# Adding the expert rows by accumulating gathers instead of a gather and an addition on VectorE

## The reference, cut to what matters

```python
x = x + gat_with_relations(layernorm(x), src, dst, edge_type)     # L0 gnn
x = x + ffn0(layernorm(x))     # the argmax expert of 32: relu(relu(x W1 + b1) W2 + b2)
x = x + gnn1(layernorm(x))
x = x + ffn1(layernorm(x))     # the top 2 of 8 experts

def gnn1(x, edge_index):       # only the first n edges count, one per node
    xt = (x @ weight).reshape(n, 4, 64)
    row, col = edge_index
    alpha = softmax(leaky_relu(alpha_l(xt[row]) + alpha_r(xt[col])), axis=1)
    tmp = einsum('nh,nhd->nd', alpha[:n], xt[col[:n]])
    return broadcast(tmp over the 4 heads)
```

## Time and profile before

| | us |
|---|---|
| median of 3 runs | 3166.9 (3164.47 to 3168.32) |
| the profiled execution | 3159.72 |
| its span | 3158.1 |
| VectorE busy | 1782.5 (56%) |
| Pool busy | 1590.8 (50%) |
| TensorE busy | 2201.9 (70%) |
| ScalarE busy | 1326.0 (42%) |

### The profile page before, as it was taken

How to read it: one execution, slowest core, us unless ns; L and a number is a source line. 1 busy time by engine, 2 the same in 40 slices (tenths; PEclk the granted TensorE clock), 3 DMA queues, 4 the chain that set the end, 5 groups by cost and what they waited for, 6 DMA issues and landing times. The chain is left out here.

```text
span 3158.1 us, 49641 instructions
## 1 busy us (share of the span) xinstructions
PE 2201.9 (70%) x13093; PEld 1863.9 (59%) x13094; DVE 1782.5 (56%) x4090; ACT 1326.0 (42%) x2973; POOL 1590.8 (50%) x1585
## 2 busy tenths in 40 slices
PE   7999966777777777777628069620700099999998
PEld 6888855565666555565517057410700088888887
DVE  2411026777777777776585524656753456556564
ACT  3444445555655555565402025310211444444443
POOL 0047337777777777777450443657047033333433
PEclk8999977888888888887765569765555599999999
DMA  6456466777765555555724135632212622222331
GB/s 187 152 194 232 186 220 200 210 211 205 213 178 144 145 145 143 143 145 131 73 83 119 53 118 176 144 66 51 83 61 101 235 42 47 49 47 45 48 50 24
DMA packets 213447, 402.41 MB, mean 127 GB/s; under 512 B 46139, under 2 KB 141096, under 8 KB 206639
## 3 DMA queue, kind: packets, MB, share of 16 engines
q0 software_dynamic: 84864, 206.63, 27.9%
q1 hardware_dynamic: 127278, 193.40, 18.8%
q10 hardware_dynamic: 1168, 0.79, 0.1%
HBM read 247.26 MB, written 155.68 MB: 128 GB/s over the span
## 5 line engine op out<-in xcount | busy, mean ns | idle before, releaser
L788 POOL DMA_INDIRECT sum_ring<-h_tab,gnn_edge_row x880 | 840.3, 955 | 267.9 <-issue 260.6
L1049 PE MATMUL sum_bank<-sum_ring,sum_one_hot 128*128 128x264 f32 x1760 | 580.7, 494 | 208.8 <-issue 191.7
L1049 PEld LDWEIGHTS sum_bank<-sum_ring,sum_one_hot 128*128 128x128 f32 x1760 | 418.1, 247 | 327.1 <-issue 222.5
L1875 POOL DMA_INDIRECT out_dram<-moe_y,moe_to_node x112 | 186.6, 1666 | 383.1 <-ACT moe_y L1901 352.1
L699 PE MATMUL rows_bank<-rows_w_rows,rows_xnT 128*128 128x264 f32 x1568 | 363.0, 391 | 6.8 <-ACT rows_h_rows L495 6.7
L699 PEld LDWEIGHTS rows_bank<-rows_w_rows,rows_xnT 128*128 128x128 f32 x1568 | 298.1, 193 | 56.7 <-ACT rows_h_rows L495 7.6
L838 ACT ACTIVATE sum_distance_by_lane<-all_iota,gnn_minus_local 128x128 bf16<-128x128 f32 x880 | 267.4, 386 | 0.1
L904 DVE TENSOR_TENSOR sum_ring<-sum_ring,sum_bank 128x1024 f32<-128x1024 f32 x220 | 265.7, 1209 | 0.4 <-ACT sum_ring L852 0.4
L1038 PEld LDWEIGHTS sum_bank<-gnn_dst_half,sum_one_hot_T 128*128 128x128 f32 x1760 | 229.9, 208 | 42.8 <-issue 39.3
L1038 PE MATMUL sum_bank<-gnn_dst_half,sum_one_hot_T 128*128 x1760 | 235.0, 292 | 27.1 <-ACT sum_one_hot_T L831 14.4
L2033 PE MATMUL moe_bank<-moe_w_low,moe_hidden_high 128*128 x896 | 244.4, 273 | 0.0
(11 more groups left out here) (408 smaller groups left out, 4164.2 us busy)
## 6 DMA issues: line engine op xcount, KB each, us to landing
h_tab<-rows_h_rows SPq DMA_DIRECT2D x49, 1056.0 KB, 3.9
sum_local_rows<-local_tab SPq DMA_DIRECT2D x110, 256.0 KB, 3.8
sorted<-sum_blank_row SPq DMA_DIRECT2D x49, 387.0 KB
moe_stage<-in_L_ffn_W_dram SPq DMA_DIRECT2D x16, 1024.0 KB
moe_tile<-sorted POOLq DMA_DIRECT2D x58, 258.0 KB, 4.2
sum_ring<-h_tab,gnn_edge_row POOLq DMA_INDIRECT x880, 3.8
sorted<-sum_zero SPq DMA_DIRECT2D x49, 256.0 KB
mask_tab<-rows_masks POOLq DMA_DIRECT2D x7, 1560.0 KB, 7.2
```

The lines of the kernel that those rows point to most:

```text
L788: nc.gpsimd.indirect_dma_start(ring[:, t % (RING * ST), :], None, k.h_tab, bass.IndirectOffsetOnAxis(k.edge_row[:, t:t + 1], 0)).then_inc( ...
L1049: last = nc.tensor.matmul(sum_b[j][:, 0:W0], hot[:, m % 2, t, :], ring[:, m % RING * ST + t, :], start=(u == 0), stop=(u == G - 1))
L1875: nc.gpsimd.indirect_dma_start(a["out"], bass.IndirectOffsetOnAxis(to_node[:, n % 2, h:h + 1], 0), y[:, n % 2, h, :], None, bounds_check=N ...
```

## The change

The buffer `y`, the semaphore `node_ok` and VectorE's `add` are gone. The gather writes to `k.x` itself, with `compute_op=ALU.add`, and is held back by the statistics of the tile eight before it. The statistics wait for the gather's semaphore.

```diff
-        y = s.sb("expert_rows", [P, SLOTS, D])
...
             for t in range(NT):
                 m = P if t < NT - 1 else TAIL
                 if t >= SLOTS:
-                    pool.wait_ge(node_ok, t - SLOTS + 1)
-                nc.gpsimd.indirect_dma_start(y[0:m, t % SLOTS, :], None, k.ys0, bass.IndirectOffsetOnAxis(k.rows0[0:m, t:t + 1], 0)).then_inc(brought[t % SLOTS], 16)
+                    pool.wait_ge(stat_ok, t - SLOTS + 1)
+                nc.gpsimd.indirect_dma_start(k.x[0:m, t, :], None, k.ys0, bass.IndirectOffsetOnAxis(k.rows0[0:m, t:t + 1], 0),
+                                             compute_op=ALU.add).then_inc(brought[t % SLOTS], 16)
...
-            def add(t):
+            def stats(t):
                 v.wait_ge(brought[t % SLOTS], 16 * (t // SLOTS + 1))
-                m = P if t < NT - 1 else TAIL
-                nc.vector.tensor_tensor(k.x[0:m, t, :], k.x[0:m, t, :], y[0:m, t % SLOTS, :], ALU.add).then_inc(node_ok, 1)
-
-            def stats(t):
-                v.wait_ge(node_ok, t + 1)
                 nc.vector.bn_stats(k.stats[:, t, :], k.x[:, t, :]).then_inc(stat_ok, 1)
...
-            add(0)
-            for t in range(1, CH):
-                add(t)
-                stats(t - 1)
-            stats(CH - 1)
+            for t in range(CH):
+                stats(t)
             variance(0)
...
-                if more:
-                    add(t1)
-                    add(t1 + 1)
                 scales(c)
                 for j in range(CH):
                     normalise(t0 + j)
                     if more:
-                        if j + 2 < CH:
-                            add(t1 + j + 2)
                         stats(t1 + j)
```

More of the change, by code:

```diff
@@ L1478, in attend1 @@
         brought = [s.sem(f"expert_rows_gathered{u}") for u in range(SLOTS)]
-        node_ok, stat_ok, var_ok, sd_ok, dve = (s.sem(n) for n in ("x_summed", "stats_ready", "var_ready", "sd_ready", "dve"))
+        stat_ok, var_ok, sd_ok, dve = (s.sem(n) for n in ("stats_ready", "var_ready", "sd_ready", "dve"))
         xn_ok, t_ps, t_ok, xt_ps = (s.sem(n) for n in ("xn_ready", "xnT_in_psum", "xnT_ready", "products_in_psum"))
```

## The result

The changed kernel takes 3178.59 us in the median of 9 runs (3172.0 to 3190.59), the kernel before 3166.9 in the median of 9 (3152.49 to 3168.32). The ratio is 1.0048, 95% interval 1.0034 to 1.0062: slower by 11 to 20 us. Predicted was 3177.5, +10.6, range 3162 to 3188. The profiled executions span 3158.1 and 3176.4 us. I write H for the time from Pool's first expert gather to its first gather of the second half: 101.2 us before (1979.09 to 2080.32), 118.9 after. That is 17.6 of the 18.3 us between the two spans. H is read from one profiled execution of each kernel; two such readings of the changed kernel, on two chips, are 118.9 and 117.9 (experiment 9), so a difference of about 1 us in H means little.

What follows compares the result with a forecast made beforehand. Pool's gather issue was to bound the stage at 1.905 us per gather; gather 48's issue, landing and 2.0 us to the root put the last root +10.6 later. Added to the 3166.9 median: 3177.5 us, range 3162 to 3188.

Steps and rivals of the forecast that it cites:

- Pool's price: In the first half of `attend1`, Pool's issue of an adding gather takes 1.605 us, against 0.95 for a plain one.
- Pool sets the pace: From chunk 2 on the gathers, 1.905 us each on Pool, set the pace and everything else follows.
- The wait for the root: VectorE's waits for ScalarE's square root, six times and 8.4 us together before, would be gone.
- VectorE's additions bring nothing: Removing 49 additions, 20.6 us of VectorE, takes 2.5 us off the path at today's pace; the gain shows nowhere.
- The landing of the last gather: Gather 48, issued at 2070.5, lands 4.2 us later at 2074.7.
- From the last root to the end: From the last chunk's square root to the end of the half, 14.25 us, nothing changes.
- the dip: Longer TensorE idling between chunks can leave it at 1.2 GHz; price 1.7 us, inside Pool's slack except in the last chunk.
- The sum: Last square root of the half at 2076.7 against 2066.07: +10.6 us, median 3177.5; chance 0.52.
- my own range: Main forecast with 1.55 to 1.67 us on Pool and a landing of 3.7 to 5.5: +7 to +15.
- 1: Pool's issue stays near plain price, 0.95 to 1.25 us, and DMA keeps up: -2.5 us, 3164.4; chance 0.26.
- rival 2: Issue cheap, but DMA engines have twice the work per row, 1.84 us per tile: +7.5, 3174.4; chance 0.10.
- 3: DMA engines pay as for the adding scatter plus contention, 2.23 us per tile: +26, 3193; chance 0.12.

Runs made afterwards that it cites:

- experiment 9: Changed kernel unedited, on a chip where the kernel before takes 3567 us: median 3579.7 against 3567.4, ratio 1.0008, H 117.9.
- experiment 7: Kernel before with a bounds check on its plain expert gathers, on a slower chip: H 116.1, no ratio given.
- experiment 4: Kernel before with gathers adding into its zeroed ring, VectorE's additions kept: ratio 1.0066, H 120.3.
- experiment 2: Changed kernel with gathers that overwrite the node rows instead of adding: ratio 0.9995, H 97.0.
- experiment 1: Changed kernel with the last tile's 106 rows gathered in two parts of 96 and 10: ratio 1.0050, H 114.1.
- 3: Changed kernel with gathers not adding and a Pool memset of 480 columns before each: ratio 1.0035, H 110.2.
- 5: Changed kernel with gathers not adding and a Pool memset of 570 columns before each, on a slower chip: ratio 1.0004, H 114.2.
- 6: Changed kernel with the 106-row gather issued ahead of tile 14's, on a slower chip: ratio 1.0007, H 115.3.
- 10: Changed kernel with the 106-row gather issued ahead of tile 14's, on another slower chip: ratio 1.0031, H 115.3.

## Why the prediction was right, and where its sizes were off
- **Pool's price**: right. Taken as 1.605 from the adding scatter, measured 1.549. Experiment 7 shows the reason for the choice to be right too: the check is 0.05 of it. The rule of the Trainium skill, two source reads and so twice the read descriptors (Collectives: The Full Stack, Part 3, The bandwidth ceiling), has the trace with it in direction: 7776 packets and not 2544 for the same bytes, and an issue of 1.55 us for 0.95. How much of the issue is the second read no run separates.
- **Pool sets the pace**: right. VectorE waits 40.9 us for the gathers, where it waited 11.1 before; Pool waits for VectorE 1.5 us in all. The wait for the root is not gone, as I had said it would be: it is 6.0 us for 8.4.
- **VectorE's additions bring nothing**: right (experiment 4). What they could have brought was put at 2.5 us, experiment 2 has 4.2.
- **The landing of the last gather**: wrong in size. I took the landing of a full tile, 4.2 us; it took 11.1. (The 4.2 holds 0.3 us "to the semaphore" that no row shows by itself; the first seven adding gathers, with no stores beside them, landed after 3.8, the median of all is 5.1.) The profile before had most of it, as the longest landing of the earlier trace rows, 8.5 us, hidden since tile 48 was wanted only 11.7 us after its issue (2060.78, at the last addition). I had read the median and the minimum. The Trainium skill has a rule that fits: DMA: Bandwidth & Descriptors (Why a DMA increments its semaphore by 16 and not by 1) says that the engines used are the largest number up to 16 that divides the slowest dimension of both sides, with an exception for some direct copies; it names no indirect DMA. For 106 rows this is 2, for 96 it is 16. The trace agrees, with a DMA share of 0.15 to 0.17 at the end, of which two engines would be 0.125, and with experiment 1.
- **From the last root to the end**: 2.2 us too little. TensorE idles 8.4 us ahead of the last chunk, for 2.1 before, and starts it at 1.2 GHz, the dip that I had named for this chunk but not put in the sum. Experiments 2, 3 and 4 idle 2.1 us there, keep the clock at 1.00 and take 14.2 to 14.4 us for this stretch; 1, 5 and 9 idle 3.4 to 8.1 us, start at 0.50 and take 15.3 to 16.6. The idle time is not the whole of it: 6, 7 and 10 idle 2.1 us too, their clock falls to 0.50 two to four us after the root, and they take 15.7 to 15.8.
- **The sum**: +10.6 predicted; -2.1 for Pool's faster issue, +6.9 for the landing, +2.2 for the clock are 17.6, what H shows. That is outside my own range of +7 to +15. The medians differ by 11.7, the ratio by 15 (11 to 20): that the predicted median came within 1.1 us is luck, not the sum.
- **Rivals**: 1 falls with Pool's 1.55 us; experiment 7 takes its reason away, and experiment 2 shows that it would have been true at 0.95. 2 and 3 fall as bounds: the engines pay 1.06 + 0.55 = 1.61 us per tile (22.0% x 116 / 46 = 0.55 for the stores), below Pool's 1.86. The work per gather grew 1.6 times, not the 2 of rival 2. It shows in the landing where nothing else runs: 3.8 us for 2.8 in the first seven gathers, of which Pool's instruction is 0.6. The median of all landings rose from 3.8 to 5.1 too, but it is 5.0 and 5.3 in experiments 2 and 3, where nothing is added, so this is not the adding's work.

## What to carry to other kernels
An addition in the DMA is not free of the engine that issues it: before taking 0.4 us per tile off an engine that has slack, look whether Pool, which gets 0.6 us per tile more, has as much. A transfer that is hidden today has its true length in the profile all the same: if the change lets the pace go over to the queue it stands in, look up the landing of the very transfer that will be last (here 8.5 us, 11.1 once it adds), not the median. And a saving on an engine that waits is worth only what stands between its wait and the next hand-over, here 2 to 4 of 20 us.

## What the runs showed of the hardware that was not expected
- A gather of 106 rows that adds keeps Pool for 2.76 us and lands after 11.1, one of 96 takes 1.47 and one of 128 takes 1.55; without adding, 106 rows take 1.57 for 0.95 and land after 8.5.
- A bounds check costs Pool 0.05 us per indirect DMA; adding costs 0.60.
- An adding gather seems to go in single packets of a row, where a plain one joins four: 7776 packets for 2544. Before, some 1560 packets are between 2 and 8 KB, a quarter of the 6250 rows of 1 KB; after, none is. An adding gather takes the DMA engines 1.6 times as long, in this company.
- The same kernel takes 3166 us on one chip and 3567 on another, and a change of 15 us in one stage that is clear on the first can't be told from none on the second (ratio 0.9979 to 1.0037).
